# Two rank-2 cross convolutions: the last T2 chunks of a block moved into the next block's S1 groups, four-array T2 in the last block, x issued ahead of stores

## The reference

```python
ret = einsum('BGMTS,GMN->BGNTS', x, w + eye)
ret += einsum('BGITS,BTGIM->BGMTS', einsum('BGMTS,BTGIM->BGITS', x, qw1), qw2)   # per row, rank 2
ret += einsum('BGITS,BSGIM->BGMTS', einsum('BGMTS,BSGIM->BGITS', x, kw1), kw2)   # per column, rank 2
ret += x * qdd[row] + x * kdd[column]
```

## Time and profile before

| | us |
|---|---|
| median of 3 runs | 790.45 |
| lowest, highest | 783.79, 791.59 |
| the profiled execution | 784.83 |
| its span, first to last instruction | 783.0 |

### The profile page before, as it was taken

How to read it: one execution, slowest core, us unless ns; L and a number is a source line. 1 busy time by engine, 2 the same in 40 slices (tenths; PEclk the granted TensorE clock), 3 DMA queues, 4 the chain that set the end, 5 groups by cost and what they waited for, 6 DMA issues and landing times.

```text
span 783.0 us, 42554 instructions
## 1 busy us (share of the span) xinstructions
PE 687.3 (88%) x18448; PEld 634.9 (81%) x18448; DVE 541.5 (69%) x769; ACT 499.1 (64%) x929; POOL 485.2 (62%) x456
## 2 busy tenths in 40 slices
PE   7378899888998999988998989979999789988976
PEld 2368889887887888978897988969989779988975
DVE  4375667475875758756785667757786567957797
ACT  7246577565776667755776657757777557765753
POOL 2257777566665766657765666647866467656632
PEclk9669999999999999989999899999999999999999
DMA  7982559942896529855499437975399545992055
GB/s 165 204 283 58 138 200 340 270 112 77 310 324 198 132 83 349 269 185 144 157 339 265 126 111 269 315 231 129 111 355 277 175 132 188 335 272 61 9 210 215
DMA packets 78567, 159.08 MB, mean 203 GB/s; under 512 B 42048, under 2 KB 43072, under 8 KB 76224
## 3 DMA queue, kind: packets, MB, share of 16 engines
q1 hardware_dynamic: 78408, 156.59, 63.3%
HBM read 87.22 MB, written 69.34 MB: 200 GB/s over the span
## 4 chain that ended last, share of the span: by engine, by line
PE 65%; SPq 9%; DMA 9%; issue 8%; DVE 7%; ACT 0%; DVEq 0%; ACTq 0%
PE PB L796 22%; PE PB L748 15%; PE PA L767 14%; PE PA L725 14%; DMA X<-in_x_dram 8%; SPq L281 5%; DVE OUT L638 3%; DVE WB L243 2%; DVE Y L614 2%; SPq L277 1%; SPq L265 1%; SPq L272 1%; SPq L284 1%; DMA products<-RT 1%; SPq L261 1%
## 5 line engine op out<-in xcount | busy, mean ns | idle before, releaser
L796 PE MATMUL PB<-Y,WB 128*128 128x128 f32 x2048 | 268.8, 281 | 9.5 <-DVE OUT L638 8.2
L796 PEld LDWEIGHTS PB<-Y,WB 128*128 128x128 f32 x2048 | 242.4, 188 | 22.7 <-issue 15.4
L614 DVE TENSOR_TENSOR Y<-PB,Y 128x512 f32 (+1 forms) x256 | 165.1, 689 | 107.4 <-PE PB L748 88.2
L454 ACT ACTIVATE Y<-PA 128x512 f32<-128x512 f32 (+1 forms) x256 | 146.5, 631 | 132.3 <-PE PA L725 132.1
L243 POOL TENSOR_TENSOR WB<-RT,mask 128x512 f32<-128x512 f32 x128 | 143.0, 1117 | 111.4 <-PE PB L796 107.7
L725 PE MATMUL PA<-X,WA 64*64 64x64 f32 x8192 | 165.2, 231 | 45.5 <-DMA X<-in_x_dram 24.9
L462 ACT ACTIVATE X<-PA 128x512 f32 (+1 forms) x256 | 140.4, 606 | 98.4 <-PE PA L767 98.3
L725 PEld LDWEIGHTS PA<-X,WA 64*64 64x64 f32 x8192 | 146.1, 143 | 64.9 <-DMA X<-in_x_dram 27.5
L235 POOL TENSOR_TENSOR WA<-RS,mask 128x512 f32<-128x512 f32 x128 | 133.5, 1043 | 85.4 <-PE PA L767 53.2
L748 PE MATMUL PB<-X,WB 64*64 64x128 f32 x4096 | 162.8, 281 | 19.7 <-issue 14.1
L235 POOL TENSOR_TENSOR WA<-RT,mask 128x512 f32<-128x512 f32 x128 | 140.2, 1098 | 61.6 <-PE PA L725 27.2
(11 more groups left out here) (33 smaller groups left out, 87.4 us busy)
## 6 DMA issues: line engine op xcount, KB each, us to landing
X<-in_x_dram SPq DMA_DIRECT2D x128, 512.0 KB, 5.6
out_dram<-OUT SPq DMA_DIRECT2D x128, 512.0 KB, 4.4
RT<-products SPq DMA_DIRECT2D x120, 128.0 KB, 3.3
products<-PROD SPq DMA_DIRECT2D x16, 128.0 KB, 7.7
Y<-in_right_dram SPq DMA_DIRECT2D x8, 128.0 KB, 8.5
X<-in_right_dram SPq DMA_DIRECT2D x8, 128.0 KB, 11.3
RT<-products SPq DMA_DIRECT2D x8, 96.0 KB, 5.0
QP<-in_rows_dram SPq DMA_DIRECT2D x8, 80.0 KB, 3.9
```

The lines of the kernel that those rows point to most:

```text
L454: nc.scalar.activation(rows_of(Y, k, j)[:, :, WIDE * h:WIDE * (h + 1), :].rearrange("q a s c -> q a c s"), PA[HALVES * (j % RING) + h][:, ...
L614: nc.vector.tensor_tensor(at, by_columns(PB[HALVES * (g % RING) + h]), at, ALU.add).then_inc(b_done, 1)
L796: last = nc.tensor.matmul(PB[g % SLOTS][:, COLS * r:COLS * (r + 1)], WB[:, g % SLOTS, P * r:P * (r + 1)], rows_of(Y, k, t2_chunk(o))[:, (i ...
```

## The change

1. `DEFER = 2`, `DEFER_AT = (0, 8)`: in every block but the last, the T phase ends with T2 chunk 13. T2 chunks 14 and 15 ("late") are computed on TensorE in the next block's S phase: chunk 14 ahead of S1 group 0, chunk 15 ahead of S1 group 8. DVE's adds, the weights and SP's store of these chunks move along; ACT's crossing stays in the T phase. T1 of the next block's chunks 14 and 15 follows T1 of chunk 13 directly.
2. In the last block T2 chunks 2, 3, 5, 6, 8, 9, 11, 12, 14 and 15 use four arrays of 64x64 (`QUARTERED_LAST`); their matrices are half as large, they need no crossing, and the host puts the halves in order. From chunk 2 on the last block's T2 matrices are made by POOL, and by ACT for the first group of each four-array chunk; DVE makes none.
3. SP issues the load of x ahead of the store of the same step.
4. The row matrices of layer 1 lie in a longer buffer RT1, with their rows in T2's order and alternating places for the last 16, so that the next block's load doesn't overwrite the late chunks' rows. Counts of semaphores are worked out from lists of work items; ACT signals once a matrix, not once a copy.

```diff
+DEFER = 2
+DEFER_AT = (0, 8)
+QUARTERED_LAST = (2, 3, 5, 6, 8, 9, 11, 12, 14, 15)
+SLOW_ROWS = CHUNK * DEFER
...
+        def s_items(k):
+            items = []
+            for g in range(GROUPS):
+                if g in DEFER_AT and not first(k):
+                    items.append(("late", CHUNKS - DEFER + DEFER_AT.index(g)))
+                items.append(("s1", g))
+            return items
+
+        def t2_chunks(k):
+            return range(CHUNKS if final(k) else CHUNKS - DEFER)
...
+        def maker(k, group):
+
+            kind, n, i = group
+            if kind == "s1":
+                return "act" if n in ACT_S1 else "pool" if n % 2 else "dve"
+            if kind == "t2" and final(k) and n >= RING:
+                return "act" if n in QUARTERED_LAST and i == 0 else "pool"
+            return "pool" if i else "dve"
...
+                for at, (kind, n) in enumerate(s_items(k)):
...
+                    if kind == "late":
+                        sp.wait_ge(b_done, added(k, at))
+                        store(k - 1, n)
...
             def t_phase(k, more, params):
-                for o in range(CHUNKS):
-                    sp.wait_ge(b_done, t2_done(k) + PER_CHUNK * (o + 1))
-                    store(k, o)
+                for o in t2_chunks(k):
+                    sp.wait_ge(b_done, added(k, item_at(k, "t2", o)))
                     if more and o + SLACK < CHUNKS:
                         load_x(k + 1, o + SLACK)
+                    store(k, o)
...
             def s_phase(k):
-
-                dve.wait_ge(a_done, s2_done(k))
-                for g in range(GROUPS):
-                    add_columns(k, g)
...
+                whole = False
+                for item, (kind, n) in enumerate(s_items(k)):
+                    if kind == "late":
+                        at = group_at(k, kind, n)
+                        add_rows(k - 1, n, used(k, at + 1), item)
+                        for i in range(PER_CHUNK):
+                            freed(k, at + i)
+                    else:
+                        if not whole:
+
+                            dve.wait_ge(a_done, s2_done(k))
+                            whole = True
+                        add_columns(k, n)
+                        freed(k, group_at(k, kind, n))
...
+            def late(k, o):
+
+                for i in range(PER_CHUNK):
+                    at, item = group_at(k, "late", o, i), item_at(k, "late", o)
+                    has_weights(k, at)
+                    bank_free(k, item)
+                    t2_group(k - 1, o, i, at, item)
...
             for k in range(BLOCKS):
                 for g in range(GROUPS + LAG):
+                    if k and g in DEFER_AT:
+                        late(k, CHUNKS - DEFER + DEFER_AT.index(g))
                     if g < GROUPS:
                         s1(k, g)
...
                 for o in range(CHUNKS):
-                    for i in range(PER_CHUNK):
-                        if o:
-                            t2(k, PER_CHUNK * o + i)
+                    if o and o in t2_chunks(k):
+                        for i in range(PER_CHUNK):
+                            t2(k, o, i)
                     if k < BLOCKS - 1:
                         t1(k + 1, o)
```

## The result

The changed kernel took 835.0 us in the median (826.6 to 842.7) against 789.4 before: a ratio of 1.0565, 95% interval 1.0504 to 1.0625. It is slower by 5.7%, where 1% faster was forecast, and outside the range of 768 to 797.

A forecast was written before the change was run, and what follows sets the result against it. PE was taken to bound T phases, its program's delivery to hold up S phases, and DVE to pace the last T phase. Last block -12, boundaries +5, small -1 gave -8: 777 on the profiled execution, 782 on the median's scale, range 768 to 797.

The forecast's parts named there:

- last block: Last T phase: with no weights on DVE from chunk 2, it ends at 768 instead of 779.85, -12 us.
- x first: x 15 sooner (bd): Block boundaries: x 15 takes the store's place in SP's queue and lands sooner, -2.0 us at each of seven.
- T2 14 ahead of S1 0: first S2 later (3.3 each): Start of S phases: T1 15 to first S2 goes from 5.95 to 9.3 us on average, +3.3 per boundary.
- T2 15 (+14) less what program waits absorb (-18): S phases: T2 15 adds 2.0 us per boundary; program waits absorb four fifths and part of the start, together 2.6.
- x first inside T phases: T phases: about 2 us of x waits besides the boundaries' go, -1; later stores stay hidden.
- Cover lost: Boundaries: T2 14 and 15 no longer fill 4.0 us ahead of T1 15; PE's wait goes from 2.7 to 4.7.
- the low clock: Boundaries: after the x wait the granted clock is at its lower level, 0.50 of full, after every boundary.
- delivery catches up: S phases: program delivery gains while PE works on a T2; "issue" waits fall from 40 to some 25 us.
- Rival 1: S phases: late T2 is paid in full, program waits do not shrink, 7 × 3.3 = +23, 800 us; chance 0.14.
- Rival 4: Boundaries: x comes no sooner than by its 0.53, +1.5 per boundary more, 792 us, no change; chance 0.15.
- PE's bare 4.4: Last T phase: PE's matmul time per three chunks without bank hand-overs, 4.4 us, giving -15 instead of -12.
- Sign (e): S phases 1 to 7 longer by about 3 us, T phases shorter by 2 to 3.

The follow-up runs named there:

- e2: The changed kernel with the stores ahead of x again: 825.1 us, ratio 1.0565.
- e3: The changed kernel with stores first and no late chunks, leaving the last block's four-array T2: 783.4 us, ratio 0.998.
- e9: The changed kernel with stores first, product stores one step later, T2 14 ahead of S1 8 and T2 15 ahead of S1 10: 787.0 us, ratio 0.998.
- e11: The same kernel as e8 run once more (no late chunks, stores first, product stores one step later): 766.5 us, ratio 0.975.
- e1: The kernel before with only SP's order changed, x ahead of the store: 808.3 us, ratio 1.031.
- e6: e1 with each store writing only its lower 64 partitions, half of the output missing: 773.6 us, ratio 0.981.
- e5: The kernel before with ten four-array T2 chunks in the last block, weights still made by DVE and POOL: 783.9 us, ratio 0.996.
- e12: The kernel before with only product stores and q one step later in SP's queue: 775.8 us, ratio 0.983.
- e8: e3 with the product stores one step later in SP's queue: 777.1 us, ratio 0.981.
- e4: The changed kernel with T2 14 ahead of S1 4 and T2 15 ahead of S1 10: 829.1 us, ratio 1.060.

## Why the prediction was wrong

Its sum, term by term, against the traces (us over the seven boundaries):

```
term, as the prediction put it                       forecast   measured
last block                                              -12       -8.5
x first: x 15 sooner (bd)                               -14      -11.9
T2 14 ahead of S1 0: first S2 later (3.3 each)          +23      +24.9
T2 15 (+14) less what program waits absorb (-18)         -4      +17.7
x first inside T phases                                  -1      +24.2
block 0                                                   0       +1.8
sum                                                      -8      +48.1
```

**Right.** Cover lost: PE's wait for x 15 went from 2.7 to 4.5 us each (4.7 forecast), and e2 shows it without the help of x first, 6.2. x 15 sooner by 1.7 us each (e2 against changed), 2.0 forecast; it landed 4.8 us after its issue in the mean, 5.9 before, 4.3 forecast. Behind six of seven boundaries T1 15 ran at the low clock (1.98 to 1.99 us; 1.17 behind the shortest wait, 3.04 us), where all seven were forecast, and the first S2 came at 9.5 us (9.3 forecast). These are three steps whose prices stood in rows of before.

**Wrong, first: the step "delivery catches up" while PE works on a T2.** It treated "issue" in S phases as a backlog that any slow stretch pays down, and took 18 us off for it. T2 15 costs 14 us by itself, and the rest grew by 17.7. "issue" at S1 and S2 was 39.9 us before and 44.5 in the changed kernel, not 25. Against kernels without late chunks and otherwise alike it is lower, 39.1 in e2 against 44.2 in e3, 36.2 in e9 against 48.4 in e11, but nothing of that reached the time: from T1 15 to the end of S2 the two late chunks, 28.7 us by themselves, cost 45 us in e2 (310.8 against 265.7) and 36 in e9. Rival 1 named this, late T2 paid in full; its ground, that the waits do not shrink at all, is a little too strong. Its price of 3.3 us a boundary, bd, S2 and T2 15 together, was (24.9 + 17.7 - 11.9) / 7 = 4.4 in the event. Why so little is absorbed is argued, not shown: if PE's sequencer held only the block in work and the next, each block would wait for its own packet, and a slow stretch would help one block only, by its own hole of some 0.6 us (39.9 us over 66 packets in S phases). The Trainium skill's "Runtime: NRT & Kernel Launch" (Instruction fetch mechanics) has the next page fetched while the current one runs, but it also gives PE room for 2048 instructions, eight blocks, so it does not decide this, and no run here shows how many are held. I had weighed its "mostly hidden" against the trace and left that sentence out of the sum. "Mostly hidden" is not what these traces show: 48 us of 783 are such waits at S1, S2 and T1 alone.

**Wrong, second: "x ahead of stores inside T phases ... -1".** The edit was priced by what x gains. What its new neighbours in the queue lose was not asked: the packets that bring PE's program are among the DMA queues, and a T phase runs them at 0.89. They start 0.6 to 0.75 us later (1.24 to 1.82 and 1.99), PE takes 256 instructions in some 5 us of a T phase and had little to spare, and 20 us more of "issue" appear ahead of T1. Of the 24.2 us in T PE stands for 15; the other 9 are longer matmul records, with the granted clock at 0.93 to 0.97 in three T phases where it was 1.00 in all seven. e1 has this alone, +22 us in time; in e6, with the stores halved, it is not there. The effect of the order itself, the same bytes one way round or the other, stays open: no run shows what on the DMA engines makes it. Rival 4 had x first in doubt, but only its benefit. No rival had it as a loss. Each of the two wrong steps would have been enough to leave the range: -1 turned to +24.2 gives 808 on the scale of the medians, -4 turned to +17.7 gives 804, and e2, with T at its old length, took 825.1.

**Mis-sized: the last block.** 30.5 us against 27 forecast, -8.5 instead of -12. DVE's waits for PE at L888 and L894 show PE's side as the limit, as said; chunk 4 is added 11.0 us behind the first add, where the working has 7.8, and that is 3.2 of the missing 3.5 us. PE stood 2.0 us there for ACT's matrix of chunk 2, the granted clock then fell to 0.50, and chunk 4's 16 matmuls took 3.78 us and not 2.05. The working had the clock in the boundaries' price and not here. Two of its figures are off without bearing on the sum: 38.5 us over 16 chunks are 2.41 each, not 2.57, and PE's bare 4.4 gives by the same steps -13 and not -15. And the reason was mis-stated: e5 has the same gain without moving a matrix from DVE. In time, e3 and e5 show 3 us each and e11 against e12 9, e8 against e12 none; what of the 8.5 arrives is not settled.

Both wrong steps lean the same way, and both rest on "issue", the one wait whose cause no row of before measured. Sign (e) shows them together: from T1 15 to the end of S2 a block takes 6.1 us more, 3 forecast, and from there to T1 15 1.8 us more, where 2 to 3 less was forecast.

## What to carry to other kernels

Before a piece of work is moved from one place to another, ask what wait it covers where it stands: here 4 us of T2 filled the wait for a load, and the load was late because 8 us of small DMAs stood ahead of it in SP's queue. The cure was to move the DMAs (one constant, 1.7%), not the work. A wait for the engine's own program was no reserve into which work could be put (e2, e4, e9); and with the DMA engines at some 0.9 a change in the order of data transfers was a change for the program's packets too (e1), so look at "issue" first.

## What was not expected of the hardware

- The order of a 512 KB load and a 512 KB store, issued 0.5 us apart with the engines at some 0.9, changes when program packets start by 0.75 us on average (1.24 to 1.99) and the kernel by 3% (e1). With the stores halved it does not (1.08 us, e6).
- "issue" ahead of S1 and S2 stays between 36 and 54 us whatever was tried: 39.9 us before, 49.0 with half the stores, 39.1 (e2) and 36.2 (e9) with 4 us of T2 in each phase, 54.1 with x first (e1), 51.8 without the wait for x 15 (e12).
- Stores that are issued second land in 5.9 to 6.0 us instead of 4.4, while x issued first gains only 0.3 in the median (5.3 in e1 against 5.6): here the one that goes second pays more than the first gains.
